# A graph network on one core: GpSimd's gathers of both edge passes, written out instead of looped

## The reference, cut to what matters

```
h = relu(layernorm(x))
# layer 1, attention over the edges (8 heads of 16)
q, k, v = projections of layernorm(h)
e[edge]   = sum(q[dst] * k[src]) / sqrt(16)           per head
alpha     = softmax of e over the edges of one dst (and a self loop)
agg[dst]  = sum over edges of alpha * v[src]
x = x + (h + agg @ Wo, then a feed-forward block)
# layer 2, a plain sum over the edges
h = relu(layernorm(x))
neigh[dst] = sum over edges of h[src]
x = x + relu(((1 + eps) * h + neigh) @ W1 + b1) @ W2 + b2
```

## Time and profile before

| | |
|---|---|
| time, median of 3 runs | 5331.64 us (5330.99 to 5337.97) |
| time of the profiled execution | 5356.35 us |
| its span, first to last instruction | 5354.7 us |
| PE busy | 520.8 us (10%) |
| DVE busy | 2791.9 us (52%) |
| ACT busy | 2153.4 us (40%) |
| POOL busy | 3544.1 us (66%) |
| instruction queue over the span | 55 packets, 0.45 MB |

### The profile page before, as it was taken

The page is one execution under the profiler, slowest core; times in us unless marked ns, Lnnn a source line. Parts: engine busy times, 40 slices in busy tenths (PEclk is TensorE's granted clock), DMA queues, the critical chain, the costliest instruction groups (busy, mean ns, idle before and its releaser), DMA issues.

```text
span 5354.7 us, 22058 instructions
## 1 busy us (share of the span) xinstructions
PE 520.8 (10%) x2377; PEld 365.8 (7%) x2377; DVE 2791.9 (52%) x4386; ACT 2153.4 (40%) x2237; POOL 3544.1 (66%) x3610
## 2 busy tenths in 40 slices
PE   4520000000000000000078100000000000000016
PEld 3310000000000000000056100000000000000004
DVE  7638887788888878878767222222222222222212
ACT  3314444444444444444356443333333333333321
POOL 4676666666666666666453677777777777777754
PEclk8665555555555555555589555555555555555557
DMA  9985555555555555555445333222222232222223
GB/s 366 374 293 182 185 198 178 186 190 193 189 185 191 186 190 190 195 182 182 145 105 111 91 104 96 93 93 92 93 92 92 94 94 94 94 94 94 94 82 115
DMA packets 235481, 816.45 MB, mean 152 GB/s; under 512 B 67005, under 2 KB 93789, under 8 KB 185242
## 3 DMA queue, kind: packets, MB, share of 16 engines
q0 software_dynamic: 143232, 344.58, 22.9%
q1 hardware_dynamic: 77464, 457.58, 22.7%
q10 hardware_dynamic: 14722, 13.70, 0.8%
HBM read 455.00 MB, written 354.21 MB: 151 GB/s over the span
## 4 chain that ended last, share of the span: by engine, by line
POOL 32%; issue 26%; DVE 21%; another core or an unknown queue 6%; ACT 5%; PE 5%; DMA 2%; ACTq 1%; POOLq 0%; SPq 0%; DVEq 0%
POOL arena L637 30%; DVE arena L1741 7%; DVE ps L1620 4%; DVE ps L1724 4%; ACT ps L1049 3%; PE ps L1310 2%; POOL q_edges L641 2%; DMA q_edges<-arena 2%; PE ps L1299 1%; DVE ps L1732 1%; ACTq L1068 1%; DVE arena L1672 1%; DVE ps L1679 1%; DVE ps L1701 1%
## 5 line engine op out<-in xcount | busy, mean ns | idle before, releaser
L637 POOL DMA_INDIRECT arena<-h_tab,idx x1568 | 1615.9, 1031 | 572.2 <-issue 552.7
L637 POOL DMA_INDIRECT arena<-kv_tab,idx x1568 | 1482.5, 945 | 762.3 <-issue 490.9
L1917 DVE SCALAR_TENSOR_TENSOR ps<-arena,keep,ps 128x128 f32<-128x128 f32 x97 | 42.4, 438 | 1669.0 <-issue 1359.6
L1187 ACT COPY ps<-arena 128x2048 f32<-128x2048 f32 x97 | 348.0, 3588 | 1122.4 <-DMA arena<-h_tab,idx 1122.4
L1083 ACT COPY arena<-arena 128x1024 f32<-128x1024 f32 x196 | 377.9, 1928 | 533.6 <-DVE arena L1741 383.4
L1620 DVE TENSOR_TENSOR_SCAN ps<-arena,ps 128x256 f32<-128x256 f32 (+2 forms) x584 | 502.1, 860 | 5.3 <-issue 3.5
L1741 DVE TENSOR_TENSOR_SCAN arena<-arena,ps 128x1024 f32<-128x1024 f32 x196 | 445.2, 2271 | 53.8 <-remote 29.2
L1194 ACT COPY arena<-arena 128x1024 f32<-128x1024 f32 x196 | 379.2, 1935 | 211.9 <-issue 137.7
L1925 DVE TENSOR_TENSOR_SCAN arena<-arena,ps 128x1024 f32<-128x1024 f32 x194 | 433.0, 2274 | 10.3 <-issue 0.5
L1049 ACT COPY ps<-arena 128x1024 f32<-128x1024 f32 x196 | 362.8, 1883 | 10.1 <-DMA arena<-q_edges 4.0
L637 POOL DMA_INDIRECT arena<-states,node_idx x196 | 190.9, 974 | 159.0 <-issue 63.2
(11 more groups left out here) (248 smaller groups left out, 2442.1 us busy)
## 6 DMA issues: line engine op xcount, KB each, us to landing
states<-arena SPq DMA_DIRECT2D x98, 1152.0 KB
q_edges<-arena SPq DMA_DIRECT2D x98, 1024.0 KB
arena<-q_edges SPq DMA_DIRECT2D x98, 1024.0 KB
states<-arena SPq DMA_DIRECT2D x98, 1024.0 KB
arena<-kv_tab,idx POOLq DMA_INDIRECT x1568
arena<-h_tab,idx POOLq DMA_INDIRECT x1568
kv_tab<-arena ACTq DMA_DIRECT2D x14, 896.0 KB
arena<-kv_tab SPq DMA_DIRECT2D x14, 448.0 KB
```

The source lines that it names most:

```text
L637: pool.indirect_dma_start(to, None, tab, bass.IndirectOffsetOnAxis(ap=at, axis=0)).then_inc(done, 16)
L1187: nc.scalar.copy(rows_now, rows[k].rearrange("p b f -> p f b")).then_inc(rows_turned, 1)
```

## The change

For both edge passes, GpSimd's loop is replaced by a plain Python loop over all 49 turns, so that every batch's gathers and waits are written out, the waits against constants; the `settle` behind the waits is dropped. Order, number, sources and targets of the gathers stay as they are, and no other engine's program is touched.

```diff
                     pool.wait_ge(idx_set, n + 1)
                     if not first:
                         pool.wait_ge(weighed_s, (n - 1) * 2)
-                    settle(pool)
                     for b in range(B):
                         gather(kvb[k][:, b, :], kv_tab, idx[k][:, b:b + 1], aside_in if last_batch(n) and b < BH else kv_in[k])
-            repeat(pool, BPAIRS, batch_b, tail=1)
+            for i in range(BPAIRS):
+                batch_b(i, i == 0)
...
                     pool.wait_ge(idx1_set, n + 1)
                     if not first:
                         pool.wait_ge(rows_turned, n - 1)
-                    settle(pool)
                     for b in range(B):
                         gather(rows[k][:, b, :], h2_tab, idx[k][:, b:b + 1], rows_in[k])
-            repeat(pool, BPAIRS, batch_d)
+            for i in range(BPAIRS):
+                batch_d(i, i == 0)
```

## The result

The changed kernel takes 5348.25 us (median of 20 runs) against 5330.47 us before (20 runs): ratio 1.0035, 95% interval 1.0026 to 1.0045. It is slower by 0.35%, some 18 us. The forecast was no change, 5331 us with a range to 5345.

The account below looks back on a forecast made before the run. GpSimd's gathers were taken to bound pass D, while B's chain goes through DVE and ACT. The terms summed to 0 in both passes, so 5331 us was forecast, range 5316 to 5345.

Parts of the forecast that it names:

- no change: Likeliest case, whole kernel: 5325 to 5340 us, chance 0.76; 0.80 for reading as no change after the rivals' shares.
- What bounds the kernel: GpSimd's gathers bound D at 22.1 us a batch; B's chain goes through DVE and ACT.
- What the change removes: GpSimd's loop instructions and increments, 12.7 us in B and 10.8 in D, hidden by its lead: 0 taken for both.
- Where the wait goes: In B `idx_set` rides on the gather, `weighed_s` keeps its instruction and 0.80 us: 0 taken, at most 13.0 us faster.
- What it adds: Written-out GpSimd code in B and D, near 38 more packets: 0 taken, at most 82 us; up to 6 us in B.
- How the numbers follow: Range 5316 to 5345 us; chances faster 0.10, same 0.80, slower 0.10; 0.02 either side for B's pattern shifting over 10.7 us.
- The rivals: Three cases for the whole kernel: no change 0.76, waits free GpSimd sooner 0.13, code arrives late 0.11.
- The faster one: `weighed_s` rides in B or the loop's work was in the way: 5308 to 5320 us, chance 0.13.
- The slower one: Code arrives late at GpSimd in D, or behind a release in B: 5342 to 5413 us, chance 0.11.

Follow-up runs that it names:

- the repeat: The changed kernel run again beside the kernel before, on another chip: 4817.69 against 4820.12 us, ratio 0.9999.
- four instructions a gather: Changed kernel with three increments of the unused semaphore ahead of every gather in both passes: 5437.89 us, 1.0155 to the kernel before.
- ACT held up: 14 copies with drains ahead of every second B batch's exponential; kernel before 5400.51 us, changed kernel 5423.28, changed kernel with `weighed_s` riding 5442.20.
- the four kernels with B written out: Against the kernel before: B alone written out 1.0024; both passes with increment kept 1.0029, with `weighed_s` riding 0.9998, released late 0.9986.
- the late release looped: Kernel before, both passes looped, eight more increments behind B's waits: 0.9998 and, run again, 1.0003, both on 4820 us chips.
- the 64 increments ahead of B: 64 increments once ahead of pass B, on the kernel before and on both passes written out with increment kept; 1.0000 and 1.0002, on 4820 us chips.
- `weighed_s` riding: Changed kernel with B's two waits in the other order, `weighed_s` first: 5331.81 us, 0.9998 to the kernel before; 1.0000 on a 4820 us chip.
- the late release: Changed kernel with eight increments between B's waits and its first gather: 5323.11 us, 0.9986 to the kernel before; with sixteen, 0.9997 on a 4820 us chip.

## Why the prediction was wrong

*What bounds the kernel.* Right for D, on every chip. One reading in it was half of the matter: that gathers are stretched to 1.93 us while DVE scans. In the kernel before, 162 of D's 178 gathers over 1.1 us do lie beside a scan. But in the repeat D has the same scans and its slowest gather takes 1.062 us, and with four instructions a gather it is 1.066 us on a 5330 us chip. So a scan alone does not stretch a gather, and what it takes besides is not shown.

*What the change removes.* Right: 0 in D, as D takes 2167.0 us against 2167.7. GpSimd's lead is even longer now: L944's last instruction comes at 5108.1 us, and the first gather of that batch at 5118.18, 10.1 us ahead in place of 8.3. In B too nothing was gained, as forecast.

*Where the wait goes.* Right: the first wait rides, `weighed_s` keeps its instruction, the release is at 0.77 us. But the 0.80 us of the earlier trace rows is the shortest release of the pass, not a typical one (median 1.09 us), so the 0.54 us saved at each was too small: from 1.05 to 0.27 it is 0.78 us. The price of the other order, 13.0 us, looks right beside the 12.4 us measured on one chip, but that is luck. DVE's wait for rows fell by 32.1 us where the prediction let at most 13.0 reach DVE, two sets of 12 runs give the 12.4 only roughly (an estimate from their spread: 5 to 21 us), and with ACT held up the sign was the other one.

*What it adds.* Right that no packet's arrival shows on GpSimd; the count was too high, 38 against 25. By the measured packets it is 3,340 instructions over 25, some 130 a packet, where the prediction took 80 to 100. It had divided by DVE's busy instructions alone; DVE's waits are instructions too, which is the likely reason.

*How the numbers follow.* This is the step that failed. The prediction allowed that "a shift of some tenths of a microsecond in GpSimd's releases could lengthen or shorten it by some microseconds", and gave 0.02 on either side to a shift beyond 10.7 us. In truth a shift of a few hundredths came with 18 us. The value taken for B, 0, was a value for GpSimd, carried over to a pass that GpSimd does not bound. The sum had no term for what the change could do to the other engines or to B's order of long and short batches, although B is bound by no single engine, and the row that says so was at hand: "another core or an unknown queue" with 9.8% of B's chain, time for which no work of the kernel accounts. The waits of L1756 would have shown it: 28 waits of 85.0 us in all in the kernel before (and 11 more of 31.7 us), on an instruction that waits for its own engine. Between the four kernels with B written out the medians lie 21.6 us apart (5344.72 to 5323.11) with releases only 0.5 us apart, and the relation is not monotonic: 0.27, 0.77 and 1.34 us give 1.000, 1.002 and 0.999. So on such a chip a difference of 0 at GpSimd bounds the program's time to within some 20 us at best, and neither the range nor the 0.80 for no change was earned.

*The rivals.* The faster one's mechanism did not happen. The slower one named late code, in D or behind a release in B; the loss was not in D, and no gather was seen waiting for code in either pass.

*What stays open.* Why the program with B written out falls out longer at an unmoved release (1.0029); the cause is not shown. Either the written-out code has a cost that acts on other engines in an episode of slow sequencer instructions, or each small change of GpSimd's timing only draws another order of batches. That ACT's copies of the hold-up idle 28 us more with GpSimd written out fits both. The kernels made to tell them apart (the late release looped, and the 64 increments ahead of B) never ran on a 5330 us chip. What makes those chips take 0.7 us for a branch is not shown by any run either.

## What to carry to other kernels

Before an edit off the critical path is costed at nothing, look at what fixes the pace of the stretch: where one engine is the bound with a lead of several instructions, as GpSimd in D, nothing short of the lead shows, but where no engine is and the batches come in two lengths, an edit that moves them by a few tenths of a microsecond or less came out anywhere from 18 us slower (1.0035) to some 7 us faster (0.9986). Look for an instruction that waits for its own engine and stands idle longer than its neighbours, and for one short sequencer instruction with two lengths (a branch of 45 or 692 ns, a drain of 276 or 977); they tell that the stretch is paced by something the program doesn't hold. Do not locate such a loss by one profiled execution of each kernel: single executions of B lay 31.5 us apart, more than the loss. Run the change on more than one chip: this one is 0.35% slower or nothing at all. Two written-out versions lost nothing there on either kind: `weighed_s` riding (0.9998 and 1.0000) and the late release (0.9986; with eight increments it did not run on a 4820 us chip, with sixteen it was 0.9997). The riding one still lost with ACT held up.

## What the hardware showed that was not expected

The same program takes 4820 us on some chips and 5330 us on others. On the latter, steps of a sequencer take about 0.70 us, or 0.70 us more, in episodes: SP's branches, 692 ns in the median against 45, ACT's drain, 977 against 276, and GpSimd's increments where there are three to a gather, 0.70 us against 17 ns. A gather that took at most 1.06 us took up to 1.95, and DVE stood up to 3.7 us behind its own previous result. With those three increments a gather, all but the increments themselves was nearly back to the short times. GpSimd pauses 2.0 to 2.2 us at every 112th gather of D on both kinds, 13 times in the pass.
